# A first tile table from partial counts, and the last router batch moved into the expert stage

## The reference

```python
Wh = x @ W                                  # x is the layer-normed input
e = leaky_relu(e_src[:, None] + e_dst[None, :], 0.2)
h = softmax(where(mask, e, NEG_INF), axis=1) @ Wh      # mask from adj, 4096 x 4096
x = x + h
# expert part, on layernorm(x) = xt
top_p, top_idx = top_k(softmax(xt @ Wr + br), 2);  weights = top_p / top_p.sum()
xe = xn[None] * ln_g[:, None] + ln_b[:, None]          # xn: xt normed again
y = gelu(xe @ W1 + b1) @ W2 + b2                       # for each expert
x = x + (weights * y[the two chosen experts]).sum()
```

## Time and profile before

| | |
|---|---|
| median of 3 runs | 1043.34 us (1040.3 to 1043.71) |
| profiled execution, its own time | 1043.86 us |
| its span, first to last instruction | 1042.2 us |
| busy: PE / DVE / ACT / POOL | 957.5 / 795.3 / 613.7 / 629.6 us |
| mean granted TensorE clock | 0.973 |

### The profile page before, as it was taken

The page is one execution under the profiler, slowest core; times in us unless marked ns, Lnnn a source line. Parts: engine busy times, 40 slices in busy tenths (PEclk is TensorE's granted clock), DMA queues, the critical chain, the costliest instruction groups (busy, mean ns, idle before and its releaser), DMA issues. The chain is left out here.

```text
span 1042.2 us, 23264 instructions
## 1 busy us (share of the span) xinstructions
PE 957.5 (92%) x7590; PEld 805.6 (77%) x7591; DVE 795.3 (76%) x1246; ACT 613.7 (59%) x924; POOL 629.6 (60%) x630
## 2 busy tenths in 40 slices
PE   5878999999999999999999708999999999999994
PEld 4767899888988889888998606777777777777773
DVE  6769998999999999999996144666576675766653
ACT  3778889888888788888885203343433434334341
POOL 2231242186573965748675252688887888878753
PEclk9999999999999999999999858999999999999998
DMA  8457778868787886878773557852232322323221
GB/s 263 93 152 199 238 252 230 266 199 266 237 244 273 228 259 221 255 257 242 256 223 121 212 165 258 248 114 50 45 56 41 51 51 43 58 41 45 40 42 21
DMA packets 92225, 170.82 MB, mean 164 GB/s; under 512 B 19952, under 2 KB 69360, under 8 KB 83824
## 3 DMA queue, kind: packets, MB, share of 16 engines
q1 hardware_dynamic: 57296, 133.00, 38.7%
q0 software_dynamic: 24048, 26.23, 16.1%
q10 hardware_dynamic: 10800, 10.52, 3.2%
HBM read 136.91 MB, written 41.19 MB: 171 GB/s over the span
## 5 line engine op out<-in xcount | busy, mean ns | idle before, releaser
L1067 ACT ACTIVATE hf<-tp,b_cols 128x256 f32<-128x256 f32 (+1 forms) x312 | 116.0, 459 | 187.3 <-PE tp L852 183.3
L748 PE MATMUL acc<-wh,pt_hi 128*128 128x256 f16 x768 | 209.3, 273 | 0.0
L749 PE MATMUL acc<-wh,pt_hi 128*128 128x256 f16 x768 | 209.3, 273 | 0.0
L750 PE MATMUL acc<-wh,pt_lo 128*128 128x256 f16 x768 | 209.3, 273 | 0.0
L517 POOL TENSOR_TENSOR x_late<-x_late,wsp 128x1024 f32<-128x1024 f32 x32 | 83.7, 2616 | 187.7 <-DMA x_late<-in_L_ffn_W 179.3
L866 PE MATMUL acc<-w_sb,h_hi 128*128 x568 | 170.9, 379 | 5.2 <-issue 3.9
L628 POOL DMA_INDIRECT out<-y_sb,yidx x71 | 118.0, 1662 | 93.2 <-DVE y_sb L1478 45.8
L1201 DVE SCALAR_TENSOR_TENSOR sc<-t_row,s_col 128x2048 f32<-128x2048 f32 x64 | 165.2, 2582 | 6.9 <-PE tp L732 5.1
L850 PE MATMUL tp<-x_hi,w_sb 128*128 128x256 f16 (+1 forms) x624 | 162.1, 265 | 2.5 <-DVE x_lo L1450 2.5
L852 PE MATMUL tp<-x_down,w_sb 128*128 128x256 f16 (+1 forms) x624 | 162.1, 265 | 0.0
L851 PE MATMUL tp<-x_lo,w_sb 128*128 128x256 f16 (+1 forms) x624 | 161.7, 264 | 0.0
(11 more groups left out here) (198 smaller groups left out, 1798.2 us busy)
## 6 DMA issues: line engine op xcount, KB each, us to landing
adj_sb<-in_adj SPq DMA_DIRECT2D x64, 1024.0 KB, 6.2
x_late<-in_L_ffn_W SPq DMA_DIRECT2D x32, 512.0 KB, 9.2
wsplit_dram<-wsp SPq DMA_DIRECT2D x32, 512.0 KB, 7.5
w_sb<-wsplit_dram SPq DMA_DIRECT2D x32, 512.0 KB, 5.9
xs<-rows_dram ACTq DMA_DIRECT2D x32, 260.0 KB, 3.2
wsp<-in_L_ffn_W POOLq DMA_DIRECT2D x32, 256.0 KB, 4.5
x<-in_x SPq DMA_DIRECT2D x32, 128.0 KB, 10.1
out<-x SPq DMA_DIRECT2D x32, 128.0 KB
```

The source lines that it names most:

```text
L748: pe.matmul(o, pt_hi[g][:, cols], wh[:, j, 0, :], start=(j == 0), stop=False)
L749: pe.matmul(o, pt_hi[g][:, cols], wh[:, j, 1, :], start=False, stop=False)
L750: m = pe.matmul(o, pt_lo[g][:, cols], wh[:, j, 0, :], start=False, stop=False)
```

## The change

The first table holds K = 12 full tiles and comes from the counts of SEEN = 5 router batches (20 token tiles). At least 20 full tiles' worth of rows are known by then, and rounding down for 8 experts leaves at least 12 (the assertion). DVE computes it in four parts (`see`) in token tiles 24 to 27. The other 27 places (FL = FT - K) are the second table's, whose segments start behind the tiles already taken (`u` of each expert).

- ACT loads tiles 0 to 3 at the end of its step for token tile 30 (`load_first`), after the scatters of batches 0 to 4 have landed.
- The engines' attention loops end at tile 31. PE does ffn_t(0), av(31, 2), ffn_t(1), av(31, 3), up(0). DVE does split_x(0), then the rest of tile 31, then split_x(1). It now waits for all stored weights ahead of split_x(1).
- POOL does index(0) and index(1), then the row scales of batch 7, gates and scatters of batch 6. Gates of batch 7 come in step 3 of the expert stage, its scatters in steps 4 and 5.
- Batch 7: ACT normalises after gelu(0) and takes exp in step 2. PE's router transposes and products stand in step 1 around the two halves of up(2), the positions in step 3. DVE's part stands at the ends of steps 1, 2 and 3.
- The second table is computed by DVE at the ends of steps 4 to 7; ACT waits for it, for all scatters and the zeroed tails in step 8, POOL in step 10, PE in step 11.
- `tiles` writes out 12 tiles instead of 4 ahead of the loop.
- SP loads expert 0 as soon as the last masked scores are done, experts 1 and 2 behind tile 30's copies, 3 behind tile 31's, and the others behind the end of attention, in each case one expert after another. All eight zeroing DMAs are SP's.
- The SBUF layout puts `xs`, `xg`, `x_hi`, `x_lo`, `x_down` and small tiles in the place of `adj_sb`, and `w_sb` behind them.

```diff
+    SEEN = 5
+    K = 3 * XR
+    FL = FT - K
+    assert SEEN * RB * P * 2 // R - E + 1 >= K
...
         def tiles(eng, body):
-            for t in range(XR):
+            for t in range(K):
                 body(t // XR, t % XR)
-            with eng.Fori(1, NB // XR - 1) as o:
+            with eng.Fori(K // XR, NB // XR - 1) as o:
...
+            def load_expert(e):
+                for q in range(CHUNKS):
+                    j = e * CHUNKS + q
+                    sp.wait_ge(s_wst[q], 16 * (e + 1))
+                    sp.dma_start(w_sb[:, j * 2 * CW:(j + 1) * 2 * CW], wsplit_dram[j]).then_inc(s_we[e], 16)
+            def expert_back(e):
+                sp.wait_ge(s_we[e], 16 * CHUNKS)
+                sp.sem_inc(s_wr, CHUNKS)
+            store_w(T - 3)
             sp.wait_ge(s_b, T)
+            load_expert(0)
+            store_x1(T - 4)
+            store_w(T - 2)
+            load_expert(1)
+            store_x1(T - 3)
+            load_expert(2)
+            store_w(T - 1)
+            store_x1(T - 2)
+            expert_back(0)
+            sp.wait_ge(s_t, G * (T - 1))
+            load_expert(3)
+            store_x1(T - 1)
+            expert_back(1)
+            load_expert(4)
+            sp.wait_ge(s_av, G * T)
+            for e in range(2, E):
+                expert_back(e)
+                if e + 3 < E:
+                    load_expert(e + 3)
...
@@ gpsimd
-            for i in range(T + RB + 1):
+            for i in range(T):
                 attend(i)
-            gates(NBATCH - 1)
-            for k in range(RB):
-                scatter_rows(NBATCH - 1, k)
...
+            scatter_rows(NBATCH - 3, RB - 1)
+            for h in range(2):
+                pool.wait_ge(s_mk[h], T)
+            pool.wait_ge(s_tab0, 1)
...
+                t = XR * o + k
+                if at(t, K - 2):
+                    pool.wait_ge(s_tab, 1)
...
+                if at(t, 3):
+                    gates(NBATCH - 1)
+                if at(t, 4) or at(t, 5):
+                    for j in range(2):
+                        scatter_rows(NBATCH - 1, 2 * (t - 4) + j)
             index(0, 0, 0)
             index(1, 1, 0)
+            row_scales(NBATCH - 1)
+            gates(NBATCH - 2)
+            for j in range(RB):
+                scatter_rows(NBATCH - 2, j)
@@ tensor
-            pe.wait_ge(s_tab, 1)
-            for r in range(RING):
-                pe.wait_ge(s_sc[r], 32 * T // RING)
+            pe.wait_ge(s_tab0, 1)
             ffn_t(0, 0, 0)
+            av(T - 1, 1, 2)
             ffn_t(1, 1, 0)
+            av(T - 1, 1, 3)
             up(0)
...
+                if at(t, 1):
+                    pe.wait_ge(s_xg, 3)
+                    router_t(b, 0)
+                    up(t + 1, 0, HC // 2)
+                    router_mm(b, 0)
+                    router_t(b, 1)
+                    up(t + 1, HC // 2, HC)
+                    router_mm(b, 1)
...
+                if at(t, 3):
+                    router_pos(b)
                 down(t, k % 2)
@@ scalar
+            def load_first():
+                act.wait_ge(s_tab0, 1)
+                for r in range(RB):
+                    act.wait_ge(s_sc[r], 32 * ((SEEN + 1) // 2))
+                    act.wait_ge(s_sc[RB + r], 32 * (SEEN // 2))
+                for h in range(2):
+                    act.wait_ge(s_mk[h], T)
+                for t in range(XR):
+                    load_x(t, t, 0)
...
             scaled(0)
             scaled(1)
+            act.wait_ge(s_wsp, T)
             gelu(0, 0)
             gelu(0, 1)
+            for j in range(RB):
+                normalise(NBATCH - 1, j)
...
+                if at(t, 2):
+                    gate_exp(b)
+                if at(t, K - XR):
+                    act.wait_ge(s_tab, 1)
+                    for r in range(RING):
+                        act.wait_ge(s_sc[r], 32 * T // RING)
+                    act.wait_ge(s_tail, 16 * E)
@@ vector
+            def see(part):
+                if part == 0:
+                    dve.wait_ge(s_slot, SEEN)
+                    link(dve.scalar_tensor_tensor(out=had, in0=iota_e[0:1, :], scalar=-float(REGION), in1=count[0:1, :], ...))
+                    link(dve.tensor_scalar(as_int, had, -R / 2 + 0.5, 1.0 / R, ALU.add, ALU.mult))
+                    link(dve.tensor_copy(full, as_int))
...
+                if RB * (SEEN + 1) <= i < RB * (SEEN + 1) + 4:
+                    see(i - RB * (SEEN + 1))
...
+            split_x(0)
+            row_sum(T - 1, 1)
+            row_reciprocal(T - 1)
+            choose_rows(NBATCH - 2)
+            add_attention(T - 1, 1)
+            stats1(T - 1)
+            moments1(T - 1)
             dve.wait_ge(s_b2, 16)
+            dve.wait_ge(s_wsp, T)
+            for q in range(CHUNKS):
+                dve.wait_ge(s_wst[q], 16 * E)
             split_x(1)
             split_h(0, 0)
...
                 result(t, k)
+                if at(t, 1):
+                    logits(b)
+                    largest(b)
+                    experts(b)
+                    keep_top(b)
+                if at(t, 2):
+                    one_hots(b)
+                if at(t, 3):
+                    choose_rows(b)
+                    dve.wait_ge(s_slot, NBATCH)
+                    dve.tensor_copy(tail_row[0:1, :], count[0:1, :]).then_inc(s_tail_in, 1)
+                if at(t, 4):
+                    table_counts()
+                if at(t, 5):
+                    table_segments()
+                if at(t, 6):
+                    table_places()
+                if at(t, 7):
+                    table_rows()
```

More of the change, by code:

```diff
@@ L205, in build @@
         yidx = [sb(f"yidx{r}", [P, S], U32, ffn_stack) for r in range(XR)]
+        small = sb("small", [P, 16 * E], F32, ffn_stack)
+        sb("pad", [P, PAD], F32, ffn_stack)
+        w_sb = sb("w_sb", [P, E * CHUNKS * 2 * CW], F16, ffn_stack)
+        w_blocks = w_sb[:, :].rearrange("p (b z n) -> p b z n", z=2, n=CW)
+        hf = sb("hf", [P, HC * R], F32, ffn_stack)
+        h_hi = [sb(f"h_hi{u}", [P, HC * R], F16, ffn_stack) for u in range(2)]
+        h_lo = [sb(f"h_lo{u}", [P, HC * R], F16, ffn_stack) for u in range(2)]
+        y_sb = [sb(f"y_sb{u}", [P, S, D], F32, ffn_stack) for u in range(2)]
+        tb = sb("tb", [P, (2 * NSEG + 5) * FL], F32, ffn_stack)
         ffn_stack.close()
@@ L308, in build @@
         TOP = 4
+        SEE = [0, 3, 6, 8]
         def halves(t):
@@ L817, in _ @@
             pe.wait_ge(s_whh, T)
-            for i in range(T + RB):
+            for i in range(T):
                 attend(i)
@@ L1368, in _ @@
                 late_lo(j)
-            for i in range(T + RB):
+            for i in range(T):
                 attend(i)
-            choose_rows(NBATCH - 1)
-            dve.wait_ge(s_slot, NBATCH)
-            dve.tensor_copy(tail_row[0:1, :], count[0:1, :]).then_inc(s_tail_in, 1)
-            dve.wait_ge(s_t, G * T)
+            NL = NB - K
             link, n = chain(dve, s_ds, base)
-            cnt, half, pair_n, odd, all_odd, end2, twice = (small[0:1, k * E:(k + 1) * E] for k in range(7))
+            cnt, half, pair_n, odd, all_odd, end2, twice, u = (small[0:1, k * E:(k + 1) * E] for k in range(8))
@@ L1413, in _ @@
-            ex, row, past, place, late = (tb[0:1, (2 * NSEG + k) * FT:(2 * NSEG + k + 1) * FT] for k in range(5))
-            pairs = cum[:, E - 1:E]
-            dve.tensor_scalar(place[:, 0:NB], iota_t[:, 0:NB], 2.0, None, ALU.mult)
-            link(dve.tensor_scalar(end2[:, 0:1], pairs, float(2 * NB), None, ALU.min))
-            link(dve.tensor_scalar(late[:, 0:NB], place[:, 0:NB], pairs, 1024.0, ALU.is_ge, ALU.mult))
-            link(dve.tensor_tensor(place[:, 0:NB], place[:, 0:NB], late[:, 0:NB], ALU.add))
@@ new lines, in _, with table_counts @@
+            ex, row, past, place, late = (tb[0:1, (2 * NSEG + k) * FL:(2 * NSEG + k + 1) * FL] for k in range(5))
+            pairs = cum[:, E - 1:E]
+            place_of = place.rearrange("o (a t) -> o a t", a=1).broadcast_to([1, NSEG, FL])
+            cum_of = cum.rearrange("o (e a) -> o e a", a=1).broadcast_to([1, NSEG, FL])
+            jump_of = jump_n.rearrange("o (e a) -> o e a", a=1).broadcast_to([1, NSEG, FL])
+            def table_counts():
+                link(dve.scalar_tensor_tensor(out=cnt, in0=iota_e[0:1, :], scalar=-float(REGION), in1=count[0:1, :], op0=ALU.mult, op1=ALU.add))
+                link(dve.tensor_scalar(as_int, cnt, P / 2 - 0.5, 1.0 / P, ALU.add, ALU.mult))
+                link(dve.tensor_copy(half, as_int))
+                link(dve.tensor_scalar(as_int, half, -0.5, 0.5, ALU.add, ALU.mult))
+                link(dve.tensor_copy(pair_n, as_int))
+                link(dve.scalar_tensor_tensor(out=odd, in0=pair_n, scalar=-2.0, in1=half, op0=ALU.mult, op1=ALU.add))
+                link(dve.tensor_reduce(all_odd[:, 0:1], odd, mybir.AxisListType.X, ALU.min))
```

(2 more changed lines are left out.)

218 lines of the change are left out of this document (104 added, 114 removed).

## The result

The changed kernel took **1008.01 us** in the median (1006.25 to 1010.89, four runs), the kernel before beside it 1042.86 us. The ratio is 0.9668 (95% interval 0.9647 to 0.9689): 34.6 us less, where 38 were forecast. The interval alone is 2.2 us to either side. The profiled execution has a span of 1006.7 us, where the sum had 1004.1.

What follows compares the result with a forecast made beforehand. PE was taken to bound both attention and expert stages, with an idle hole between. 1042.2 - 42.9 + 3.0 + 0.5 + 1.3 = 1004.1 us of span, some 1005 in the median; range 1000 to 1015.

Steps and rivals of the forecast that it cites:

- Part 1: Between attention and expert stage: PE's hole closes, up(0) at 589.3, up(1) at 596.3 instead of 639.22; gain 42.9 us.
- covers: Before up(0): attention matmuls hide ACT's scaling (1.0 us) and DVE's split (1.5 us); early loads hide the weights' arrival.
- Part 2: Last batch's router work moves between PE's expert matmuls: +3.0 us, and +0.5 for waits on ACT's copies.
- Part 3: First table's thirteen DVE operations in token tiles 24 to 27, 2.7 us: half taken to reach PE, +1.3 us.
- Part 4: Expert stage: added router, second-table, table-load and zeroing work on DVE, ACT and SP fits their waits; costs nothing.
- Part 5: Expert stage: POOL's gates and 16 scatters, 1.6 us each, make it late, catching up 1.5 us per tile; cost 0.
- at most 11: Expert stage, step 5: the most that POOL was forecast to run late, in us.
- The margin of 14: Expert stage: POOL may be up to 14 us late before PE misses an accumulator, 11 plus another 3.
- rival A: Expert stage: row scatters wait for DVE, POOL's backlog passes 14 us, PE waits for an accumulator; 1008 to 1018, chance 0.18.
- Rivals B and C: B: hole closes only in part, 1015, worst 1025, chance 0.08. C: every row scatter takes 4.4 + 0.3 us, 1050, chance 0.04.
- B's second mechanism: Start of expert stage: DVE's new waits for stored weights hold split_x(1), so the hole closes only in part.

Runs made afterwards that it cites:

- e4: Changed kernel with both last attention groups of tile 31 first, then the transposes of tiles 0 and 1; 1012.80 us, ratio 0.9704.
- e5: Changed kernel with SP's loads of the expert weights held until attention has ended; 1029.27 us, ratio 0.9828.
- e1: Kernel before plus the first table's thirteen small DVE operations in token tiles 24 to 27, result unused; ratio 1.0033, +3.4 us.
- g2: Changed kernel with twelve of the thirteen first-table operations moved to token tile 31, run beside the changed kernel; 1005.41 us, ratio 0.9614.
- f1: Changed kernel with twelve of the thirteen first-table operations moved to token tile 31, an earlier run; 1007.69 us, ratio 0.9636.
- e6: Changed kernel with 40 linked 128 x 8 operations added on POOL at the end of step 5 to delay it; 1019.76 us, ratio 0.9747.
- h1: Changed kernel with the first table's second part moved from token tile 25 to tile 24; 1007.56 us, ratio 0.9665.
- e7: Changed kernel with 120 linked 128 x 8 operations added on POOL at the end of step 5 to delay it; 1029.92 us, ratio 0.9844.
- e3: Changed kernel with up(0) ahead of tile 31's last attention group, and DVE, POOL and SP reordered to suit; ratio 0.9720.
- e2: The changed kernel run again without an edit; 1006.89 us, ratio 0.9656.

## Why the forecast held, and where it was off

**Part 1 held.** From the end of attention on, the forecast's times are met: up(0) directly behind attention, up(1) 7.2 us after it (7.0 forecast), clock 1.00, and no wait for weights or tiles. Its covers were real: e4 shows 2.3 us under the interleaved attention, e5 18 us of waits if the weights are asked for 31 us later.

**Part 2 held.** From up(1) to the end took 1006.7 - 600.82 = 405.9 us against 1042.2 - 639.22 = 403.0: +2.9, where 3.0 + 0.5 stood. In the chain of waits of the changed kernel the moved router work stands between expert matmuls with the durations of the earlier trace rows:

```profile
614.92 0.79 PE rt_ps L794 x8
615.72 0.49 PE xt_ps L783 x4
```

**Part 3 was mis-sized.** The step "some of which will meet idle time of DVE: I take half" failed. In the kernel before DVE is busy for 72.0 of the 75 us from 455 to 530, so there was little idle time to meet, and about the whole 2.7 us went through: +3.4 us of time in e1, 4.9 and 2.7 us back when the operations moved (g2 and f1). The traces say it from tile 25's masked scores on, which start ahead of the table's first operation in every profile. From there to tile 31's takes 96.6, 98.0 and 96.6 us without the table in it (before, f1, g2; mean 97.1) and 98.2 to 101.3 with it (eleven profiles, mean 99.3): 2.3 us. In the profiled execution that I forecast it was 99.2, 2.6 more than before.

**The rest of the miss lies ahead of the table's first operation**, at 470.13 in that execution. Tile 24's masked scores started 3.8 us late there (441.30 against 437.53), tile 25's 2.2 us late (457.34 against 455.15). PE's waits up to 437 us show 1.0 us at the first transposes (12.3 against 11.3 us, for DVE's first rows), 1.3 more for DVE's one-hots and 1.2 more for ACT. The first is in every other profile too (12.1 to 12.5), e1 among them, so it tells of the one profile of before. The others vary from 2.7 to 5.5 us in sum among kernels that are alike up to tile 24 (2.7 and 5.2 in f1 and g2, which are one kernel), while before and e1 have 2.9 and 2.1. Whether the new layout of the buffers has a share in that stays open.

One source of such differences can be seen. In the kernel before, in tile 24:

```profile
448.21 2.12 POOL L517 TENSOR_TENSOR x_late<-x_late,wsp 128x1024 f32<-128x1024 f32 x1 [5.42 <-DMA x_late<-in_L_ffn_W]
448.27 2.11 DVE L1289 TENSOR_TENSOR oh<-iota_e,idxf 128x32 f32<-128x32 f32 x1
```

DVE's operation takes 0.19 us elsewhere. Here tile 25's masked scores came 17.6 us after tile 24's. In four profiles (the changed kernel's, e6, f1, g2) the product met no small operation there, and they came after 16.0 us; in eight others one was stretched to between 1.78 and 2.16 us, and they came after 17.2 to 18.1 us (h1: 1.16 and 16.5). From tile 29's to tile 30's it is 15.4 to 15.5 us in ten profiles, and 16.5 in the four (e1, e4, e7, h1) in which the scores met the product and took 4.2 us. So 1 to 2 us of difference between executions come with which operation of DVE POOL's product meets.

So the span comes out as the forecast 1004.1, plus 2.2 that had arisen by tile 25, plus 1.3 of part 3 (2.6 where 1.3 stood), less 0.1 for the transposes (the stretch from tile 31's masked scores to the end of attention grew by 0.9, not 1.0), less 0.4 because up(0) began 0.16 us ahead of attention's modelled end and not 0.2 behind it, plus 0.2 from up(0) to up(1), less 0.6 of part 2: 1006.7. By the times of all executions the gain was 3.7 us smaller than forecast, of which e1's 3.4 for 1.3 explains 2.1; the other 1.6 is less than the result's interval.

**Part 4 held.** The second table's longest part ran on DVE from 683.38 to 687.8, and the split of the next tile's rows began at 687.82 with nothing of PE late. The table loads for the last gates took 1.28 us each (633.64 and 638.92), inside ACT's idle time. ACT's first copy after the tile loads came at 574.64, after 1.0 us of waiting for scatters to land and 4.3 us of issuing the four loads; that is 2.1 us late against the kernel before (1.5 forecast), and it cost nothing either.

**Part 5: the outcome held, the way to it in part by luck.** Late by "at most 11": 10.5. The 16 row scatters took 1.31 us in the mean; with the 0.30 us ahead of each that is the 1.6 that was taken. But the gates took 6.0 us (654.03 to 659.98) where 2.8 stood, and yet tile 4's scatter was only 0.2 us late; tile 5's two y scatters took 2.32 and 3.38 us; and tiles 7 to 10 were still 9.3, 9.3, 9.1 and 8.1 us late, where 1.5 us per tile was to be caught up. These errors nearly cancelled at tile 6. The margin of 14 is 15.1 to 15.3. Of it 4.7 us were left, so rival A was close enough to be worth its 0.18: e6 shows what 10 us more would have cost. Rule of the Trainium skill (SBUF — State Buffer, "SBUF: two separate sides"): an operation that takes the port pair shared by DVE and POOL holds it to its end, and the other waits. These runs agree in both directions (the 4.30 us scores beside POOL's 2.13; scatters of up to 2.02 us beside DVE in the expert stage). What made rival A fail is not the rule but its reach: 10 of the 16 scatters took no more than 1.08 us, and the mean is what adds up.

**Rivals B and C** didn't come about, but B's second mechanism exists: it showed in e5, where the last store was issued 18 us later. How much less would do was not tried.

## What to carry to other kernels

When a second engine is nearly as busy as the one that bounds the kernel, small operations put on it can cost their full sum, as here: price them at the upper bound, or look for the tile in which that engine idles, which here was seven tiles further on and gave the best version (2.7 and 4.9 us under the changed kernel in two comparisons). Work moved beside a bound engine is free up to a margin that can be read from the trace: next use of the buffer, less landing time, less the latest issue; two runs that delay it on purpose then give the margin (here 14 by the sum, 15.1 to 15.3 measured) and what lies beyond it. A delay that comes out as forecast can still be a sum of wrong terms. And before blaming a stretched operation, look whether another one was stretched in the same place before.

## What the runs showed of the hardware

- In three kinds of places an operation of DVE that started with POOL's 128 x 1024 product (2.12 to 2.15 us) took about 2 us longer, whatever its size: 2.18 us for 8 elements (0.15 alone), 2.12 for a cast of 128 x 8 (0.16), 4.30 for the scores (2.34).
- The other way: one of POOL's 128 x 8 operations (row scales) took 1.68 us in the changed kernel and 3.73 in e3, where it lay beside DVE's split of the hidden tile.
- The indirect scatters of batch 6 had a mean of 1.42 us and at most 2.02 (600 to 615 us, DVE busy for 11.1 of 15), those of batch 7 a mean of 1.21 (665 to 689 us, DVE busy for 21.8 of 24); in other executions one of them took 2.75 (e2, e7, h1). Under the 4.42 us masked operation of the attention stage it was 4.39.
- PE's clock fell after short waits too: with one of 5.35 us the mean was 0.83 in the 20 us around it (e6), with one of 19.99 us 0.74 and 0.75 in two windows of 20 us (e7), between the 2.4 and 1.2 GHz levels (a granted clock of 1.00 and 0.50). After the 1.84 us ahead of up(1), and the 1.33 and 1.00 us of e4, the windows show 1.00.
